# Attention's output projection: four-pass fp32 products replaced by three fp32r products, split three groups later, and moved one group on

## The reference, cut to what matters

```
q = (x @ Wq + bq)  -> 16 heads of 32        k = x @ Wk + bk        v = x @ Wv + bv     # one key/value head
attn = softmax(q @ k.T / sqrt(32))          out = attn @ v         # heads side by side again: 512 columns
return out @ Wo + bo                                               # the output projection
```

## Time and profile before

| | |
|---|---|
| runs | 3183.83, 3176.17, 3182.91 us; median 3182.91 |
| profiled execution | 3182.29 us, span 3180.6 us, mean granted clock 0.934 |
| PE, PEld | busy 87% and 52% of the span |
| DVE, ACT, POOL | busy 64%, 48%, 70% |
| attention's groups | from 822 to about 2509 us, PE busy throughout |
| chain that ended last | 2% of the span: only the last stage's loads |

### The profile page before, as it was taken

One profiled execution on the slowest core, in us unless ns is written; L12 is line 12 of the kernel. 1 busy time (PEld: TensorE's weight loads), 2 busy tenths in 40 slices (PEclk: granted clock), 3 DMA queues, 4 the chain that ended last, 5 costly groups with the idle time before them and its releaser, 6 DMA issues. The chain is left out here.

```text
span 3180.6 us, 44938 instructions
## 1 busy us (share of the span) xinstructions
PE 2770.0 (87%) x15264; PEld 1651.1 (52%) x15264; DVE 2046.3 (64%) x3922; ACT 1522.7 (48%) x2871; POOL 2218.7 (70%) x1430
## 2 busy tenths in 40 slices
PE   7967777388899999999999999999999776888870
PEld 4644444166455555555555555555554464555540
DVE  7843222267788878788787887887874394333334
ACT  5522222153466656566566665665656351222220
POOL 2248888462489879799798897997978323777770
PEclk9978888689999999999999999999999877999995
DMA  5669999895377777678676776776766364999998
GB/s 211 220 198 244 237 241 242 184 272 189 83 157 161 144 159 147 137 170 160 143 162 134 167 144 139 164 150 155 148 135 140 121 219 135 212 236 240 236 184 322
DMA packets 216987, 575.78 MB, mean 181 GB/s; under 512 B 33980, under 2 KB 35004, under 8 KB 192824
## 3 DMA queue, kind: packets, MB, share of 16 engines
q0 software_dynamic: 87296, 343.98, 53.7%
q1 hardware_dynamic: 125240, 220.55, 21.4%
q10 hardware_dynamic: 4224, 8.39, 0.7%
HBM read 230.94 MB, written 155.24 MB: 121 GB/s over the span
## 5 line engine op out<-in xcount | busy, mean ns | idle before, releaser
L1914 DVE TENSOR_REDUCE attention_mx<-attention_pM 128x1 f32<-128x512 f32 x1984 | 1209.3, 682 | 197.0 <-PE attention_pM L1797 196.3
L1744 ACT ACTIVATE attention_prob<-attention_pS 128x512 f32<-128x512 f32 x2048 | 1032.7, 624 | 592.2 <-PE attention_pS L1776 591.8
L1691 POOL TENSOR_TENSOR attention_pair<-attention_prob 128x1024 f32<-128x1024 f32 x380 | 949.6, 2504 | 210.0 <-ACT attention_prob L1744 199.3
L1776 PE MATMUL attention_pS<-attention_qT,prep_kT 128*128 128x512 f32 x2048 | 840.6, 412 | 3.1 <-ACT attention_prob L1744 2.2
L1797 PE MATMUL attention_pM<-prep_kT,attention_qT 96*128 96x512 f32 x1984 | 788.2, 398 | 1.8 <-DVE attention_mx L1914 1.1
L1776 PEld LDWEIGHTS attention_pS<-attention_qT,prep_kT 128*128 128x128 f32 x2048 | 387.5, 190 | 308.9 <-issue 210.2
L1825 PE MATMUL attention_pO<-attention_prob,attention_v 128*32 128x512 f32 x4096 | 491.7, 598 | 0.0
L768 POOL DMA_INDIRECT sum<-experts_res,c_table x256 | 403.7, 1577 | 125.4 <-issue 79.4
L1797 PEld LDWEIGHTS attention_pM<-prep_kT,attention_qT 96*128 96x128 f32 x1984 | 377.9, 190 | 92.0 <-DVE attention_mx L1914 16.5
L752 POOL DMA_INDIRECT experts_rows<-xn_rows,c_table x256 | 250.7, 979 | 103.8 <-issue 70.1
L797 PE MATMUL experts_pT<-c_ident,experts_rows 128*128 128x128 f32 x1024 | 169.8, 307 | 120.8 <-issue 46.8
(11 more groups left out here) (181 smaller groups left out, 3135.1 us busy)
## 6 DMA issues: line engine op xcount, KB each, us to landing
prep_acc<-attention_pair POOLq DMA_DIRECT2D x96, 1024.0 KB, 7.6
attention_acc<-attention_pair POOLq DMA_DIRECT2D x90, 1024.0 KB, 7.3
attention_qT<-q_parts SPq DMA_DIRECT2D x96, 256.0 KB
xn_rows<-route_xn SPq DMA_DIRECT2D x16, 1152.0 KB, 6.6
experts_wup<-in_L_ffn_w_up_dram SPq DMA_DIRECT2D x64, 256.0 KB
q_parts<-prep_acc SPq DMA_DIRECT2D x64, 256.0 KB, 4.3
ahead_wup<-in_L_ffn_w_up_dram SPq DMA_DIRECT2D x64, 256.0 KB, 9.0
combine_got<-sum SPq DMA_DIRECT2D x16, 1024.0 KB
```

The lines of the kernel that those rows point to most:

```text
L1691: pool.tensor_tensor(to[:, part], prob[2 * n % PROBS][:, part], prob[(2 * n + 1) % PROBS][:, part], ALU.add).then_inc(s_pair, 1)
L1744: act.activation(prob[t % PROBS][:, h * QT:(h + 1) * QT], pS[:, at, :], ACT.Exp).then_inc(s_ex, 1)
L1776: pe.matmul(pS[:, n % 3, :], kT[:, key:key + P], qT[g][:, h, :], start=True, stop=True).then_inc(s_sc, 1)
L1914: dve.tensor_reduce(mx[:, unit, part:part + 1], pM[:, r % RING, :], X, ALU.max).then_inc(s_mr, 1)
```

## The change

- The raw outputs of the groups go to a ring of three tiles `raws` instead of one tile for each group, and POOL normalises them in place there.
- Three groups later, after pair 0, ACT rounds the normalised tile to fp32r (`high`, into `o_hi`) and writes its negative, rounded, into a fourth tile of `raws`. After its maxima in pair 2 DVE adds the two, pairwise (`low`: a tensor_reduce whose two inputs of each sum are 2 to 6 KB apart), which gives `o_lo`.
- `wo` is split the same way once, in groups 1 (ACT) and 2 (DVE).
- `output` makes 12 fp32r matmuls instead of four fp32 ones: high by high, low by high, high by low.
- `OUT_PAIRS` moves from pairs 4 to 7 of the second group to pairs 3 to 6 of the third. At the end of the last chunk the groups 0 to 2 go by three products, the last one by fp32 as before.
- The shifts' second part is now a sum over pairs too, with one more small reduction.
- SP's program is not touched.

```diff
-        OUT_PAIRS = (4, 5, 6, 7)
+        OUT_PAIRS = ((2, 3), (2, 4), (2, 5), (2, 6))
+        HIGH_PAIR, LOW_PAIR, RAWS = 0, 2, 3
...
+        raws = m.sb("raws", [P, RAWS + 1, QT])
+        raw = [raws[:, b, :] for b in range(RAWS)]
+        wo_hi, wo_lo = prep["wqh"], prep["wql"]
...
-            return OUT_PAIRS.index(k) if G % GPC == 1 and G > GPC and k in OUT_PAIRS else None
+            at = (G % GPC, k)
+            return OUT_PAIRS.index(at) if G > GPC and at in OUT_PAIRS else None
...
-                    if g == 0 and not (isinstance(c, int) and c == 0):
-
-                        pool.wait_ge(s_mr, A + outputs_done[c - 1])
-                        pool.sem_inc(k["pool_on"], 1)
-                    pool.tensor_tensor(o_n[g][:, :], o_raw(g)[:, :], d_rec[:, :], ALU.mult).then_inc(s_on, 1)
+                    pool.tensor_tensor(raw[G % RAWS], raw[G % RAWS], d_rec[:, :], ALU.mult).then_inc(s_on, 1)
...
+                def high(G):
+                    c, g = divmod(G, GPC)
+                    act.wait_ge(s_on, A + G + 1)
+                    if c > 0:
+                        act.wait_ge(s_mr, A + outputs_done[c - 1])
+                    act.wait_ge(s_ol, A + G)
+                    act.activation(o_hi[g], raw[G % RAWS], ACT.Copy).then_inc(s_oh, 1)
+                    act.activation(raws[:, RAWS, :].bitcast(F32R), raw[G % RAWS], ACT.Copy, scale=-1.0).then_inc(s_oh, 1)
...
+                        if t == 2 * HIGH_PAIR + 1 and G > 2:
+                            high(G - 3)
...
                     for g in range(GPC):
-                        ins = pe.matmul(pM[:, r % RING, :], o_n[g][:, t * P:(t + 1) * P], wo_sb[:, g, :],
-                                        start=g == 0, stop=g == GPC - 1)
+                        pe.matmul(pM[:, r % RING, :], o_hi[g][:, own], wo_hi[:, g, :], start=g == 0, stop=False)
+                        pe.matmul(pM[:, r % RING, :], o_lo[g][:, own], wo_hi[:, g, :], start=False, stop=False)
+                        ins = pe.matmul(pM[:, r % RING, :], o_hi[g][:, own], wo_lo[:, g, :], start=False,
+                                        stop=g == GPC - 1)
...
+                def low(G):
+                    dve.wait_ge(s_oh, A + 2 * G + 2)
+                    both = raws[:, G % RAWS:RAWS + 1:RAWS - G % RAWS, :].rearrange("p r n -> p n r")
+                    with nc.allow_low_precision(reason="what rounding leaves is exact in float32r"):
+                        dve.tensor_reduce(o_lo[G % GPC][:, :], both, X, ALU.add).then_inc(s_ol, 1)
...
+                    if G == 2 and p < GPC:
+                        low_wo(p)
+                    if p == LOW_PAIR and G > 2:
+                        low(G - 3)
```

More of the change, by code:

```diff
@@ L1495, in attention @@
         shift = m.sb("shift", [P, HG, HG, DH])
-        whole = m.sb("whole", [P, UNITS])
+        whole = m.sb("whole", [P, UNITS, 2])
         prob = [m.sb(f"prob{b}", [P, HG * QT]) for b in range(PROBS)]
@@ L1499, in attention @@
         pair = [m.sb(f"pair{b}", [P, HG * QT]) for b in range(MOVED)]
-        o_new = m.sb("o_new", [P, QT])
-        o_n = [m.sb(f"o_n{g}", [P, QT]) for g in range(GPC)]
+        raws = m.sb("raws", [P, RAWS + 1, QT])
+        raw = [raws[:, b, :] for b in range(RAWS)]
+        o_hi = [prep[n][:, :, :].rearrange("p c n -> p (c n)") for n in ("wkvh", "wkvl")]
+        o_hi += [m.sb(f"o_hi{b}", [P, QT], F32R)[:, :] for b in range(2)]
+        wo_hi, wo_lo = prep["wqh"], prep["wql"]
+        o_lo = [m.sb(f"o_lo{g}", [P, QT], F32R) for g in range(GPC)]
+        o_last = raw[(GROUPS - 1) % RAWS]
         d_sb = m.sb("d", [P, QT])
@@ L1513, in attention @@
         s_wo = m.sem("wo")
+        s_woh = m.sem("woh")
+        s_wol = m.sem("wol")
+        s_oh = m.sem("oh")
+        s_ol = m.sem("ol")
         s_xl = m.sem("xl")
@@ L1540, in attention @@
         s_shd = m.sem("shd")
-        def o_raw(g):
-            return o_new if g == 0 else o_n[g]
         def blocks_in(G, k):
@@ L1733, in _ @@
             def _(act):
-                begin(act, s_ex, s_sha)
+                begin(act, s_ex, s_sha, s_woh, s_oh)
                 def exponential(G, t, h):
@@ L1750, in copy_shift, with high_wo @@
                                    ).then_inc(s_sha, 1)
+                def high_wo(g):
+                    if g == 0:
+                        act.wait_ge(s_wo, A + 16)
+                    act.activation(wo_hi[:, g, :], wo_sb[:, g, :], ACT.Copy).then_inc(s_woh, 1)
+                def high(G):
[6 more added lines that the diff above has]
+                    act.activation(raws[:, RAWS, :].bitcast(F32R), raw[G % RAWS], ACT.Copy, scale=-1.0).then_inc(s_oh, 1)
                 for h in (2, 3):
@@ L1757, in _ @@
                             exponential(G, t, h)
+                        if G == 1 and t % 2 == 1 and t < 2 * GPC:
+                            high_wo(t // 2)
+                        if t == 2 * HIGH_PAIR + 1 and G > 2:
+                            high(G - 3)
                         if t == 2 * COPY_PAIR + 1 and G + 1 < GROUPS:
@@ L1760, in _ @@
                                 copy_shift(G + 1, (G + 1) % GPC, h)
+                high(GROUPS - 3)
+                high(GROUPS - 2)
             @block.tensor
@@ L1851, in last_output @@
                         pe.wait_ge(s_ex, A + GROUPS * (STEPS * HG))
+                    own = slice(t * P, (t + 1) * P)
                     if t == 0 and 0 in groups:
-                        pe.wait_ge(s_on, A + GROUPS - 1)
-                    if GPC - 1 in groups:
-                        pe.wait_ge(s_lon, A + t + 1)
+                        pe.wait_ge(s_ol, A + GROUPS - 1)
                     for g in groups:
[L1857 to L1860, removed]
+                        if g < GPC - 1:
+                            pe.matmul(last_out(t), o_hi[g][:, own], wo_hi[:, g, :], start=g == 0, stop=False)
+                            pe.matmul(last_out(t), o_lo[g][:, own], wo_hi[:, g, :], start=False, stop=False)
+                            pe.matmul(last_out(t), o_hi[g][:, own], wo_lo[:, g, :], start=False, stop=False)
+                        else:
+                            pe.wait_ge(s_lon, A + t + 1)
+                            pe.matmul(last_out(t), o_last[:, own], wo_sb[:, g, :], start=False, stop=True
+                                      ).then_inc(s_mp, 1)
                 def phase(G, p):
@@ L1908, in _ @@
             def _(dve):
-                begin(dve, s_mr, s_mx, s_shift, s_shd, s_dc, s_rec, s_oc, s_lrec, s_lon)
+                begin(dve, s_mr, s_mx, s_shift, s_shd, s_dc, s_rec, s_oc, s_lrec, s_lon, s_wol, s_ol)
                 def maxima(r, count, n):
@@ L1983, in _ @@
                         phase(G, p)
+                low(GROUPS - 3)
+                low(GROUPS - 2)
                 dve.wait_ge(s_lsum, A + PAIRS)
@@ L1994, in last_quarter @@
                         dve.wait_ge(s_pv, A + GROUPS * STEPS)
-                    dve.tensor_tensor(o_n[GPC - 1][:, part], pO[:, part], d_rec[:, part], ALU.mult).then_inc(s_lon, 1)
+                    dve.tensor_tensor(o_last[:, part], pO[:, part], d_rec[:, part], ALU.mult).then_inc(s_lon, 1)
                 def last_added(t):
```

22 lines of the change are left out of this document (14 added, 8 removed).

## The result

The changed kernel takes 3266.4 us (median of 4 runs, 3264.3 to 3267.7) against 3183.1 of the kernel before: a ratio of 1.027, 95% interval 1.026 to 1.028. It is slower by 83 us; forecast were 126, and a time between 3240 and 3360. The profiled execution has a span of 3265.5 us (before 3180.6).

A forecast was written before the change was run, and what follows sets the result against it. PE was taken to set the pace. From the profiled 3182.3 us: -24.4 (projection) + 23 (low parts) + 126 (SP's order) + 1 (small) = 3308 us, range 3240 to 3360.

The forecast's parts named there:

- part 1: Output projection on PE (also step 1): a tile 2.80 us instead of 3.60, -22.4 us for 28 tiles; with last chunk -24.4.
- step 3: Low-part reduction on DVE after pair 2's maxima: 1.90 us each, PE stalled 0.82 us 28 times, +23 (ends 4 and 34).
- the six stalls: PE standing still in pair 7 of each third group while maxima go on: 18.9 us each, 113.4 us.
- step 4: SP's queue: DVE waits 19.5 us through store, load, denominators and `d_in`; PE waits 17.1, clock and pacing 1.8; +126.
- The seventh stall: Group 30, no maxima following: late denominators hold up the output copy and POOL's normalising; 13 us, bounded by 0 and 18.9.
- step 5: Small things: one more small reduction in the shifts (0.2 us) and wo's four subtractions; +1 us, at most 10.
- The rival that POOL is held up by late denominators: Late denominators stop POOL's normalising, then ACT, then PE; 10 us more lost each time, 3378 us; chance 0.08.
- 0.85, 0.08 and 0.03: Chances: PE stalls behind SP as forecast; POOL held up as well (3378 us); three products not cheaper (3375 us).

The follow-up runs named there:

- Experiment 1: The changed kernel with SP's store of finished rows and load of the next rows one group later: 3165.5 us, ratio 0.995.
- experiment 2: The kernel before with one wait more: SP holds the store until DVE's last maxima tile of pair 6 in the third group: 3282.4 us, ratio 1.032.
- experiment 6: Experiment 1's kernel without the product of high attention output and low wo, in all chunks but the last: 3137.5 us, ratio 0.986.
- experiments 8 and 9: Experiment 1's kernel with six, then eight extra unused DVE reductions; stepped against dense: 574 against 420 ns (256 inputs by four), 1220 against 1207 (1024 by two).
- experiment 5: Experiment 1's kernel with the low parts by one addition of two SBUF operands in place of the reduction: 3174.3 us, ratio 0.998.
- experiment 4: The changed kernel with the four output tiles and the low parts one pair earlier in the third group: 3255.2 us, ratio 1.023.
- experiments 5 and 7: Experiment 5 has its own line; 7 is experiment 1's kernel with wo's four subtractions one pair later: 3162.5 us, ratio 0.994.
- experiment 3: The changed kernel with only the load of the next rows one group later, behind the denominators: 3243.5 us, ratio 1.020.

## Why the prediction was right in sign, and where its sizes were off

**Right.** The mechanism, its place and its sign: SP's store now waits for an addition that DVE makes right ahead of an instruction that needs SP. Experiment 1 takes it away and 101 us go; experiment 2 puts it alone into the kernel before and 101 us come. Busy time would not have told it: the busy shares hardly differ (PE 85% of the span instead of 87%, DVE 64% in both). That PE sets the pace elsewhere was right too (experiment 6), so part 1 was a gain in full. Of the 36 us by which the sum for attention was too high, 23 are step 3 and 20 the six stalls; the smaller errors partly cancel.

**Wrong, step 3, the low parts: +23, measured 0.** The price of 1.90 us was taken from the one stepped reduction, as "nearest in kind"; but that row sums four and the new one two, and only the former pays (experiments 8 and 9). The right row was the dense one, 1.22. By the Trainium skill, "SBUF — State Buffer", section Door 1, each access that crosses to a new line of 16 bytes pays; sums of four and sixteen agree (0.6 ns an input), sums of two do not, and there the measurement decides. The lower end of 4 us was still too high: DVE's slack is at least 1.24 us and below 1.38 (experiment 5), not 1.12.

**Mis-sized, step 4, the chain: 19.5 us, measured 15.0 to 16.7.** Its links were priced from rows in which POOL's transfers run on. In the stall POOL stands still, the store lands in 7.8 us instead of 10.9 and the denominators in 5.6 instead of 6.6. Adding up links that were each priced elsewhere is not safe either way: store and denominators took 4.6 and 8.7 in experiment 2, 8.4 and 9.6 in experiment 4. With the true chain the rest of the step holds: PE waits 13.0 where 17.1 was forecast, 4.1 less for a chain 3.9 shorter, and clock and pacing take 2.2 to the 1.8 forecast. The seventh stall came by the copy of the output, as thought. That its 11.5 us are near the 13 forecast is luck: 13 was a choice between bounds, and DVE waited 24.5 us there, longer than the chain of 19.5.

**Mis-sized, step 1: 0.80 us a tile, measured 0.58** ((14.37 - 12.03) / 4). Twelve matmuls at 0.233 are 2.80, as said; but the first begins 0.44 us after its predecessor and the second 0.33 after it. The row that gave 2.80 leaves these passages out, since there such matmuls follow one another; the old tile's 3.60 is a difference of whole pairs and has its own passages in it. (It set pair 7 with a tile against pair 0 without one; pair 7's own 5.87 gives 3.52, and the four pairs 3.59 on average.)

**Small, step 5: +1, measured +4.4**, one collision with POOL inside the stated end of 10. The shifts' new reduction, charged with 0.2 us, removed another such collision and gave 2.0 us. The rival that POOL is held up by late denominators showed itself only in the last chunk (9.50 us, after PE had gone on). One slip in the chances: 0.85, 0.08 and 0.03 for the cases that are slower make 0.96, not 0.95.

## What to carry to other kernels

When an operation moves later, look first at every queue that waits for it and at what stands behind that wait; a store that is harmless after its data is a stall when it waits ahead of somebody's input. Price a chain of transfers as a whole, with the traffic that will run beside it then, and take a price only from a row of the same form (here: inputs in a sum, operands in SBUF). And before dropping a change that came out slower, move the one thing that blocks: here two numbers turned +83 us into -15, each against the kernel before beside it.

## What the runs showed of the hardware that was not expected

- A step between inputs costs a DVE reduction 0.6 ns an input where four or sixteen are summed, and nothing where two are (experiments 8 and 9). For sums of four the type made no difference, nor 2 KB instead of 256 bytes; sums of two, in fp32, were free at 512 bytes to 6 KB.
- A DVE operation of 128x512 on two SBUF operands ends 0.3 to 0.6 us after the end of a POOL addition that it meets, and not always the first: one waited until POOL's unbroken row of operations was over. 0.7 us at best became 1.2 to 3.8, and once 19.5 (experiments 5 and 7).
- Four stores of 2 KB and the wait for them took 2.0 us with no load ahead of them, 5.2 to 5.7 with a load of 1 MB issued just ahead, and 8.2 to 9.6 where POOL's transfer ran beside the chain as well (six stalls each of experiment 3, the changed kernel and experiment 4).
